# Emitting the first Hadamard step of the up/gate stage one loop pass later in a fused attention and FFN kernel

## The reference

```python
def _L0_ffn_ref(input, ...):
    n = SU_ug.shape[0]
    x = input.reshape(-1, n)                       # 8192 x 2048
    x = fwht(x * SU_ug) / SCALE
    x_up = x @ W_up.T * (Wscale_ug[:INTER] * SCALE)      # INTER = 8192
    x_gate = x @ W_gate.T * (Wscale_ug[INTER:] * SCALE)
    x = jax.nn.silu(x_gate) * x_up
    x = fwht(x * SU_dp) / SCALE
    x = x @ W_down.T * (Wscale_dp * SCALE)
    return x.reshape(input.shape)

x = L0_attn_x
x = _layernorm(x + _L0_attn_ref(x, ...), axis=-1)
x = _layernorm(x + _L0_ffn_ref(x, ...), axis=-1)
```

## Time and profile before

| what | us |
|---|---|
| median of 3 runs (lowest, highest) | 3281.99 (3279.12, 3553.1) |
| the profiled execution's own time | 3279.97 |
| its span, core 2, the slowest of 8 | 3278.9 |
| spans of the other cores | 3258.4 to 3278.0 |
| the up/gate stage in it, first up matmul to last copy | 1586.3 to 2610.2 |

### The profile page before, as it was taken

How to read it: one execution, slowest core, us unless ns; L and a number is a source line. 1 busy time by engine, 2 the same in 40 slices (tenths; PEclk the granted TensorE clock), 3 DMA queues, 4 the chain that set the end, 5 groups by cost and what they waited for, 6 DMA issues and landing times.

```text
span 3278.9 us, 28802 instructions; the slowest of 8 cores (3258.4 to 3278.9 us)
## 1 busy us (share of the span) xinstructions
PE 2646.5 (81%) x11024; PEld 1034.2 (32%) x11024; DVE 589.6 (18%) x626; ACT 636.3 (19%) x616; POOL 114.5 (3%) x203
## 2 busy tenths in 40 slices
PE   3999993998999999411699998999999749999970
PEld 1444441222222222100244433444444313444430
DVE  0222220111112111272111111111111140000014
ACT  0000002655655565400000000000000030000010
POOL 1000000000000000000000000000000000000000
PEclk9999996999999999755899999999999969999985
DMA  9358637001010000016444444444444393444526
GB/s 149 69 87 140 115 65 185 1 1 39 1 39 1 0 1 1 3 42 152 90 83 81 81 81 82 85 87 84 81 80 81 72 225 82 104 105 113 116 52 205
DMA packets 120421, 258.76 MB, mean 79 GB/s; under 512 B 34784, under 2 KB 75744, under 8 KB 115168
## 3 DMA queue, kind: packets, MB, share of 16 engines
q0 software_dynamic: 54960, 149.54, 27.2%
q1 hardware_dynamic: 64376, 102.13, 10.1%
q10 hardware_dynamic: 952, 5.24, 0.7%
HBM read 337.19 MB, written 58.72 MB: 121 GB/s over the span
## 4 chain that ended last, share of the span: by engine, by line
PE 76%; DMA 8%; DVE 7%; ACT 4%; issue 3%; another core or an unknown queue 1%; DVEq 0%; POOL 0%; SPq 0%; ACTq 0%; POOLq 0%
PE ps_ug L164 28%; PE ps_y L164 14%; PE ps_ring L164 14%; PE ps_o L404 7%; PE ps_d L400 6%; PE ps_s L164 5%; DVE QSB L678 2%; DMA AR<-scr_f 2%; ACT AR L457 2%; DMA ARF<-xkvA 2%; DMA ARF<-scr_f 1%; DMA out<-stg_f 1%; PE ps_rd L373 1%; DMA ARF<-xq 1%; PE ps_f L164 1%
## 5 line engine op out<-in xcount | busy, mean ns | idle before, releaser
L164 PE MATMUL ps_ug<-AR,QSB 128*128 128x512 bf16 x2688 | 586.9, 379 | 63.3 <-DVE QSB L678 63.3
L164 PEld LDWEIGHTS ps_ug<-AR,QSB 128*128 128x128 bf16 x2688 | 260.0, 98 | 390.0 <-issue 82.3
L164 PE MATMUL ps_ug<-AR,WBUF 128*128 128x512 bf16 x1408 | 309.1, 380 | 43.9 <-DVE QSB L678 32.7
L164 PE MATMUL ps_s<-QSB,AR 128*128 128x512 bf16 x768 | 237.1, 392 | 79.4 <-DMA AR<-scr_vt 47.0
L714 ACT ACTIVATE stg_b<-ps_ug,sgate 128x1024 bf16<-128x1024 f32 x64 | 71.3, 1114 | 931.5 <-PE ps_ug L164 931.5
L678 DVE CAST QSB<-ps_ug 128x1024 bf16<-128x1024 f32 x64 | 78.4, 1224 | 850.8 <-PE ps_ug L164 850.8
L164 PE MATMUL ps_y<-ARF,QSB 128*128 128x512 bf16 x1024 | 226.3, 382 | 4.2 <-issue 4.2
L164 PE MATMUL ps_ring<-ARF,AR 128*128 128x512 bf16 x768 | 170.1, 383 | 55.7 <-DMA ARF<-xkvA 55.7
L400 PE MATMUL ps_d<-AR,ones_b 128*1 128x512 bf16 x512 | 196.8, 384 | 11.0 <-DVE rowbuf L419 11.0
L164 PEld LDWEIGHTS ps_ug<-AR,WBUF 128*128 128x128 bf16 x1408 | 136.6, 98 | 216.8 <-issue 56.7
L404 PE MATMUL ps_o<-AR 128*128 128x512 bf16 x512 | 203.2, 397 | 0.0
(11 more groups left out here) (106 smaller groups left out, 1493.7 us busy)
## 6 DMA issues: line engine op xcount, KB each, us to landing
QSB<-WdownT POOLq DMA_DIRECT2D x16, 2048.0 KB, 15.4
QSB<-WupT POOLq DMA_DIRECT2D x42, 512.0 KB, 5.3
QSB<-WgateT POOLq DMA_DIRECT2D x42, 512.0 KB, 8.2
ARF<-xkvB POOLq DMA_DIRECT2D x8, 2048.0 KB, 20.5
scr_f<-QSB SPq DMA_DIRECT2D x64, 256.0 KB, 7.4
WBUF<-WupT POOLq DMA_DIRECT2D x22, 512.0 KB, 5.2
WBUF<-WgateT POOLq DMA_DIRECT2D x22, 512.0 KB, 8.0
ARF<-xkvA POOLq DMA_DIRECT2D x4, 2048.0 KB, 42.8
```

The source lines that it names most:

```text
L164: return pe_.matmul(out_ap, lhsT, rhs, start=start, stop=stop, skip_group_check=True)
```

## The change

`pend` becomes a list. In pass c, if it holds two blocks, the older one (block c-2) is taken out and `emit_stage1` is called for it at the top of the pass, ahead of the waits and matmuls of block c. The call behind the gate matmuls is dropped. After the loop, the two blocks that are left are emitted in order. Buffers, tile sizes, the semaphores and their counts for each block stay as they are.

```diff
@@ -662,7 +662,7 @@
-            pend = [None]
+            pend = []
 
             def emit_stage1(c, buf, dvv, acv):
@@ -687,6 +687,8 @@
                 pu, pg = PS[2 * pb], PS[2 * pb + 1]
+                if len(pend) >= 2:
+                    emit_stage1(*pend.pop(0))
                 p.w(pe_, ["ug0", "ug1", "ug2"][buf], wld[buf])
                 p.w(pe_, "dv", pu_free[pb])
@@ -707,8 +709,6 @@
                     wupgate_load(buf, c + 3)
-                if pend[0] is not None:
-                    emit_stage1(*pend[0])
                 p.w(ac_, "pe", pe_gt)
                 p.w(ac_, "dv", gsl_done[pb])
@@ -720,8 +720,9 @@
                 gsl_done[pb] = dvv
-                pend[0] = (c, pb, dvv, acv)
-            emit_stage1(*pend[0])
+                pend.append((c, pb, dvv, acv))
+            while pend:
+                emit_stage1(*pend.pop(0))
```

## The result

The changed kernel takes 1.061 times as long as the kernel before (95% interval 1.0592 to 1.0628), that is 200 us more: by this ratio about 3482 us against a median of 3281.79. The forecast was 3457. Its span grew from 3272.7 to 3472.8 us.

What follows compares the result with a forecast made beforehand. PE was taken to bound the kernel, waiting 62 times for a DVE copy in the up/gate stage. 3279.97 + 122 (longer waits) + 53 (clock) = 3455; median 2 us higher, 3457, range 3430 to 3490 (3400 to 3515 with rivals).

Steps and rivals of the forecast that it cites:

- First term: Up/gate stage: each of PE's 62 waits for the DVE copy grows 1.97 us, 122 us in all (119 to 138).
- the first step: Up/gate pass, inside PE's wait: from silu start on ACT to product start on DVE, 1.23 us.
- step 2: Up/gate pass, inside PE's wait: from product start to copy start on DVE, 1.19 us, bounds 1.14 and 1.44.
- The end of the stage: After the up/gate loop: last copy starts 3.56 us after last silu instead of 3.88; the 0.3 us less was neglected.
- Second term: Up/gate stage: longer waits lower PE's clock, costing 0.85 us a pass (bounds 0 and 1.71), 53 us in all.
- the 0.95 in the text: Sign for the clock cost: 53 us in a 1200 us up/gate stage would be a granted clock of about 0.95.
- The price of a stretch on matmuls: Up/gate stage: a short 1.2 GHz stretch falling wholly on a pass's 64 matmuls costs 1.71 us.
- The unchanged clock: Rival, up/gate stage: clock stays at 2.4 GHz, only silu, product and copy in series are paid; 3404 us, chance 16%.
- The full price in each pass: Rival, up/gate stage: every wait costs a full slow stretch, 106 us instead of 53; 3510 us, chance 15%.
- The rival in which the copy gets cover: Rival, up/gate stage: pair and copy run behind another block's matmuls, the 96.0 us of waits vanish; 3186 us, chance 1%.

Runs made afterwards that it cites:

- after_fill: Changed kernel plus 15 dummy PE matmuls between Hadamard pair and first up matmul, every pass from 2 on: 3401.59 us, 1.0379 of the kernel before.
- The delays: Four kernels: the kernel before plus a useless DVE addition of 440, 900, 1380 or 1870 columns ahead of the copy; ratios 1.0215, 1.0216, 1.0674, 1.0694.
- before_delay15: Kernel before plus a useless DVE addition of 1380 columns (about 1.5 us) ahead of the copy: 1.0674 of the kernel before.
- delay10_work8: Kernel before plus a useless 900-column DVE addition ahead of the copy and 8 dummy matmuls between up and gate every pass: 3536.82 us, ratio 1.0804.
- before_delay10: Kernel before plus a useless DVE addition of 900 columns (about 1.0 us) ahead of the copy: 1.0216 of the kernel before.
- gate_first: Kernel before with each block's 32 gate matmuls issued ahead of its 32 up matmuls: 3173.39 us, 0.9686 of the kernel before.

## Why the prediction was right, and where it was off

- **PE's order doesn't change, DVE's does, and the wait then holds silu, product and copy.** Right. The wait stayed at the same place and at 62 times, and the three steps stand in series in the timeline.
- **First term, 62 x 1.97 = 122 us.** Measured: 125.6, or 2.03 for each wait. The steps were 1.28, 1.20 and 1.36 us, forecast as 1.23, 1.19 and 1.37. The 0.05 in the first step is the only miss of note. The product of the stage's first block, from which 1.23 was read, waits for `ac` alone, those of the steady passes for `ac` and `pe`. In the changed kernel (core 4) the products of blocks 0 and 1, which wait for `ac` alone, start 1.23 us after their silu, and those from block 2 on 1.28 to 1.29 us; that the second semaphore is the reason fits this but wasn't tested. (In step 2 the distance from Hadamard pair to copy is 0.18 us by its own numbers, not 0.17, which moves nothing.) after_fill isolated this term at 124 us.
- **The end of the stage, 3.56 us from last silu to last copy instead of 3.88.** Right: of the changed kernel's last two copies (2805.48, 2.35 us for both) the second starts about 3.6 us after the last silu at 2802.99.
- **Second term, the clock.** That waits of 3.5 us would bring the clock down was right, and the size was too small: 53 us forecast, 71 measured, 1.15 us a pass instead of 0.85. The 0.85 was the middle between two bounds, and that it came this near is partly luck. It makes up most of the forecast's miss of 25 us in 200. The picture behind it, a slow stretch in every pass with half of it hidden in the wait, isn't what the trace shows: 24 of 62 passes run at the full clock and pay nothing, and 38 pay 1.7 to 2.7 us. Little is hidden: a clock of 0.93 over 1200 us is about 168 us at 1.2 GHz, which would cost 84 us if all of it fell on matmuls, and 71 were paid. The clock of 0.93 is the counterpart of the 0.95 in the text. The price of a stretch on matmuls (1.71) was right (1.69).
- **The reasoning under the second term** was partly wrong. It took the length of the wait as what decides: 1.55 harmless, 2.6 harmful, 3.5 in between or worse. The delays show waits near 2.0 us that lower the clock to 0.96 and waits of 2.5 that hardly do. The four waits in attention were true examples, but the threshold read into them doesn't exist as such. The changed kernel's 71 us lie within the range of 11 to 116 that waits of 2.0 to 3.5 us had in passes without dummy matmuls, and no step of the prediction could have told where.
- **The rivals.** The unchanged clock (3404) is what after_fill measured at 3401.59, but it took the filling to get there. The full price in each pass (106 us, 3510) wasn't reached by the changed kernel but was passed by before_delay15 with 116. This was also the Trainium skill's rule in "TensorE: Matmul & The Clock Gate", section "HAM oscillation — how this bites in real kernels", that each tile's wait is paid. The runs come near it in before_delay15 (59 of 62 passes longer) and delay10_work8 (55), and disagree in the changed kernel (38) and before_delay10 (7). The rival in which the copy gets cover had the right mechanism for a different edit: gate_first puts matmuls between pair and copy on one side and the tile's next use on the other, which the changed loop does not, and gains more than the 96 us of the table.

## What to carry to other kernels

Moving a call to "one pass later" defers it only on those engines that have an instruction between the old and the new place. List what stands in between for each engine: here PE had nothing, so the tile was needed as early as before, and DVE had one product that slipped in front of the copy for which PE waits. To cover such a copy, put independent work of the waiting engine behind it (the other PSUM tile's matmuls); that gained 3%, more than the idle time in the table, whichever order DVE had.

When PE waits in every pass, compare the granted clock of the stage, not only the waits: here it added 71 us to 126. Whether a wait cost that could not be told from its length in these runs, and it could be tested cheaply by filling the wait with matmuls into a tile that will be overwritten.

## What the runs showed of the hardware that was not expected

A longer wait isn't always slower. With the waits at 124.7, 154.0, 185.0 and 216.7 us in total, the clock's cost was 41, 11, 116 and 95 us, in 24, 7, 59 and 43 longer passes. With the waits fixed at 154 us and the pass lengthened by 0, 1.73 and 3.45 us of dense matmuls, it was 11, 94 and 10 us, in 7, 55 and 6. So the length of the pass decides along with that of the pause. That it does so through the moments at which PE's pauses fall is Theory E; its two forecasts held, but no run shows it directly. A pass either pays for a slow stretch, 1.3 us or more, or nothing. Which rule of the chip lies behind this was not determined by these runs. They show that it is neither the length of the pause alone nor the share of matmul work in a pass alone: the dummy matmuls raised that share twice at an unchanged wait, and the clock fell with the first 8 and rose with the second 8.

By the same reasoning the changed kernel's cost of 71 us should belong to its pass length too, and another kernel with waits of 3.5 us may pay more or less. No run changed the pass length at waits of 3.5 us.
